# Cross attention: TensorE transposes the low half of 36 units in steps without another item, the DMA their high half alone

## What is computed

```python
def _L1_xattn_ref(q, k, v, wq, wk, wv, wo):      # N_HEADS 16, HEAD_DIM 64
    qh = (q @ wq.T).reshape(B, Sq, N_HEADS, HEAD_DIM).transpose(0, 2, 1, 3)
    kh = (k @ wk.T).reshape(B, Sk, N_HEADS, HEAD_DIM).transpose(0, 2, 1, 3)
    vh = (v @ wv.T).reshape(B, Sk, N_HEADS, HEAD_DIM).transpose(0, 2, 1, 3)
    scores = jnp.einsum('bhqd,bhkd->bhqk', qh, kh) / jnp.sqrt(jnp.float32(HEAD_DIM))
    attn = jax.nn.softmax(scores, axis=-1)
    ctx = jnp.einsum('bhqk,bhkd->bhqd', attn, vh)
    ctx = ctx.transpose(0, 2, 1, 3).reshape(B, Sq, N_HEADS * HEAD_DIM)
    return ctx @ wo.T
```

## Time and profile before

| | us |
|---|---|
| median of 3 runs | 3689.03 (3686.04 to 3690.8) |
| profiled execution | 3689.56 |
| its span | 3687.8 |
| PE / DVE / ACT / POOL busy in the span | 3077.8 / 2698.4 / 2332.4 / 1058.7 |
| DMA transposes | 512 of L1998, 96 of L267 |
| mean granted TensorE clock | 0.928 of full |

### The profile page before, as it was taken

One profiled execution on the slowest core, in us unless ns is written; L12 is line 12 of the kernel. 1 busy time (PEld: TensorE's weight loads), 2 busy tenths in 40 slices (PEclk: granted clock), 3 DMA queues, 4 the chain that ended last, 5 costly groups with the idle time before them and its releaser, 6 DMA issues. The chain is left out here.

```text
span 3687.8 us, 77444 instructions
## 1 busy us (share of the span) xinstructions
PE 3077.8 (83%) x30696; PEld 1830.7 (50%) x30836; DVE 2698.4 (73%) x4017; ACT 2332.4 (63%) x4361; POOL 1058.7 (29%) x1854
## 2 busy tenths in 40 slices
PE   6999999878998755899688878998799879998823
PEld 3647474555665443444345544555455545555411
DVE  4848483777897665444379888888788888889788
ACT  3838374676786534333268877778777777788534
POOL 2232322156537235233122222222222222222122
PEclk9999999988998877999899999999999999999956
DMA  4050504266265375344399999999999999999843
GB/s 156 21 170 2 171 14 136 65 221 203 77 183 164 100 255 192 93 128 123 104 208 194 195 202 202 202 198 191 213 196 198 194 214 195 199 201 196 161 153 129
DMA packets 1346682, 591.77 MB, mean 160 GB/s; under 512 B 1181202, under 2 KB 1267858, under 8 KB 1343764
## 3 DMA queue, kind: packets, MB, share of 16 engines
q1 hardware_dynamic: 1342292, 570.03, 70.0%
q0 software_dynamic: 4032, 16.78, 1.2%
HBM read 183.63 MB, written 109.45 MB: 79 GB/s over the span
## 5 line engine op out<-in xcount | busy, mean ns | idle before, releaser
L2259 DVE SCALAR_TENSOR_TENSOR ca_halves<-ca_probs,ca_inv,ca_halves 128x1024 f16<-128x1024 f32 x512 | 655.1, 1279 | 138.8 <-ACT ca_halves L2187 132.0
L2187 ACT ACTIVATE ca_halves<-ca_probs,ca_inv 128x1024 f16<-128x1024 f32 x512 | 586.1, 1145 | 151.6 <-DMA ca_pt<-ca_halves 145.9
L2253 DVE TENSOR_REDUCE ca_neg_max<-banks 128x1 f32<-128x1024 f32 x512 | 623.1, 1217 | 65.2 <-PE banks L2056 63.5
L2179 ACT ACTIVATE ca_probs<-banks,ca_neg_max 128x1024 f32<-128x1024 f32 x512 | 567.7, 1109 | 82.0 <-DVE ca_neg_max L2253 79.3
L2056 PE MATMUL banks<-ca_kt,ca_qt 64*128 64x512 f16 x3072 | 388.7, 387 | 102.3 <-ACT ca_probs L2179 100.8
L2022 POOL TENSOR_SCALAR ca_inv<-ca_total 128x1 f32<-128x1 f32 x512 | 97.6, 191 | 1225.5 <-ACT ca_probs L2179 1225.5
L2076 PE MATMUL banks<-ca_pt,ca_v 128*64 128x256 f16 x6144 | 392.1, 278 | 18.4 <-DMA ca_pt<-ca_halves 18.4
L2076 PEld LDWEIGHTS banks<-ca_pt,ca_v 128*64 128x64 f16 x6144 | 322.3, 111 | 120.2 <-issue 104.6
L2025 POOL TENSOR_TENSOR ca_inv<-ca_inv,ca_minus_one 128x1 f32<-128x1 f32 x512 | 280.4, 548 | 42.6
L2056 PEld LDWEIGHTS banks<-ca_kt,ca_qt 64*128 64x128 f16 x3072 | 133.7, 95 | 297.5 <-issue 121.3
L2037 PE MATMUL banks<-ca_ct,ca_w 128*128 128x512 f16 x768 | 180.9, 386 | 53.0 <-DVE ca_kt L2233 29.5
(11 more groups left out here) (303 smaller groups left out, 5635.7 us busy)
## 6 DMA issues: line engine op xcount, KB each, us to landing
ca_w<-ca_w_parts SPq DMA_DIRECT2D x32, 768.0 KB, 5.6
wa_v<-v_rows SPq DMA_DIRECT2D x44, 264.0 KB, 4.6
v_rows<-wa_v_stage SPq DMA_DIRECT2D x32, 264.0 KB, 2.2
wa_x<-in_x SPq DMA_DIRECT2D x32, 256.0 KB, 5.2
wa_ring<-in_x SPq DMA_DIRECT2D x32, 256.0 KB, 3.8
x_after_window_attention<-wa_ring SPq DMA_DIRECT2D x32, 256.0 KB, 3.3
ba_tokens<-wa_tok_turned SPq DMA_DIRECT2D x32, 256.0 KB, 3.7
ba_xt<-ba_tokens SPq DMA_DIRECT2D x32, 256.0 KB, 7.4
```

The lines of the kernel that those rows point to most:

```text
L2179: act.activation(probs[:, slot, :], scores(i), ACT.Exp, bias=neg_max[:, slot:slot + 1], accum_out=total[:, slot:slot + 1]).then_inc(exped, 1)
L2187: act.activation(halves[:, slot, 0, :], probs[:, slot, :], ACT.Copy, scale=inv[:, slot:slot + 1]).then_inc(split_hi, 1)
L2253: dve.tensor_reduce(out=neg_max[:, slot:slot + 1], in_=scores(i), axis=X_AXIS, op=ALU.max, negate=True).then_inc(maxed, 1)
L2259: dve.scalar_tensor_tensor(out=halves[:, slot, 1, :], in0=probs[:, slot, :], scalar=inv[:, slot:slot + 1], in1=halves[:, slot, 0, :], op0= ...
```

## The change

In steps 2 to 255 that have no item (`flip_at`), PE transposes the low half of the last step's first unit into the spare bank, eight 128x128 pieces, once that half is written. ACT copies the bank into ca_pt one step later, ahead of its second exponential. The DMA transposes the high half alone for these units. New waits: `weigh` also waits for the copies of its units, `spare_free` for the copies before, DVE's low half of unit i for the flip of unit i - 3 (the slot), and ACT's copy for the weighing that last read this place of ca_pt.

```diff
+        flip_at = {step: 2 * (step - 1) for step in range(2, STEPS)
+                   if not any(step in busy for busy in (qk_at, v_at, tile_at, partly_at))}
+        flipped_units = set(flip_at.values())
+        low_flipped, low_placed = sem("ca_low_flipped"), sem("ca_low_placed")
+        def flips_until(unit):
+            return sum(1 for u in flipped_units if u <= unit)
...
-                            sp.dma_start_transpose(pt[:, step % 4, h, :, :],
-                                                   halves[:, i % SLOTS, :, :].rearrange("p q s -> p (q s)")
+                            parts = 1 if i in flipped_units else 2
+                            sp.dma_start_transpose(pt[:, step % 4, h, 0:parts * NT, :],
+                                                   halves[:, i % SLOTS, 0:parts, :].rearrange("p q s -> p (q s)")
                                                    ).then_inc(turned[i % SLOTS], 16)
...
+                        if flips_until(4 * g + 3):
+                            pe.wait_ge(low_placed, flips_until(4 * g + 3))
...
+                    flips = sum(1 for at in flip_at if at < step)
+                    if flips:
+                        pe.wait_ge(low_placed, flips)
...
+                def flip_low(i):
+                    bank = psum[:, SPARE, :].bitcast(F16)
+                    pe.wait_ge(split_lo, i + 1)
+                    for kb in range(NT):
+                        last = pe.transpose(bank[:, kb * P:(kb + 1) * P],
+                                            halves[:, i % SLOTS, 1, kb * P:(kb + 1) * P], consts.ident_h[:, :])
+                    last.then_inc(low_flipped, 1)
...
                 def beside(step):
+                    if step in flip_at:
+                        spare_free(step)
+                        flip_low(flip_at[step])
...
                 def high_item(step):
+                    if step in flip_at:
+                        i = flip_at[step]
+                        act.wait_ge(low_flipped, flips_until(i))
+                        if step >= 5:
+                            act.wait_ge(weighted, (step - 5) // 2 + 1)
+                        act.activation(pt[:, (step - 1) % 4, 0, NT:2 * NT, :],
+                                       psum[:, SPARE, :].bitcast(F16).rearrange("p (k c) -> p k c", c=P),
+                                       ACT.Copy).then_inc(low_placed, 1)
...
                     dve.wait_ge(split_hi, i + 1)
+                    if i - SLOTS in flipped_units:
+                        dve.wait_ge(low_flipped, flips_until(i - SLOTS))
```

## The result

The changed kernel takes 3650.15 us (median of 5 runs, 3638.95 to 3663.97) against 3686.04 (5 runs, 3675.41 to 3690.8). The ratio is 0.9902, 95% interval 0.9883 to 0.9921. The forecast was 3679 us, with a range of 3664 to 3697; the change gained some 36 us where 10 were expected. The profiled execution took 3650.15 us, its span is 3648.2.

The account below looks back on a forecast made before the run. ACT and DVE were taken to pace each other, with DMA transposes bounding about 146 of cross attention's 1624 us. Terms +8 (A), -7 (B), -11 (C) sum to -10 us against 3689.56, so 3679 us, range 3664 to 3697.

Parts of the forecast that it names:

- class B: Step 5 of twelve ordinary turns, unit 8 behind the weights: 12 flips, transpose relief 1.03 us each, sum -7 us.
- Class A: Step 2 of the same twelve ordinary turns, unit 2: 12 flips, 0.68 us of copy exposed each, no relief, +8 us.
- Class C: Four steps in a row at each of three batch ends: 12 flips, SP relieved, copies hidden, -11 us.
- What bounds the kernel: Cross attention: transposes bound about 146 of 1624 us; elsewhere ACT and DVE pace each other and pay for added work.
- Rival 1: Too small to measure, about 3688 us: queue relieved by less than 1.03 us, after large loads time is the load's; 25%.
- Rival 2: Slower, about 3701 us: ACT with its copies bounds steps 3 and 6 of the turn, no relief behind the weights; 17%.
- Rival 3: Much faster, about 3654 us: DMA engines bound every step, so 36 x 1.03 = -37 us, less little; 8%.

Follow-up runs that it names:

- e5: Changed kernel with all 36 copies sent to a scratch tile and the DMA transposing both halves as before; ratio 1.0037 to the kernel before, stage 1622.5 us.
- e2: Kernel before with flips only in step 5 of the twelve ordinary turns (12 flips); ratio 0.9966, stage 1600.7 us.
- e16: Changed kernel without the twelve flips of step 2 (24 flips left); 3659.55 us, ratio 0.9931 to the kernel before, stage 1587.2 us.
- e17: Kernel before with flips only in step 5 of ordinary turns, plus 64 idle waits on PE ahead of the stage; stage 1601.4 us, one execution.
- e6: Changed kernel without PE's and ACT's added work, 35 low halves not transposed at all; ratio 0.9888 to the kernel before, stage 1576.8 us.

## Why the prediction was wrong

The step that failed is the pricing of a halved transpose behind a large load (class B): its relief was put at 1.03 us, the difference of two undisturbed issues, where the run shows 2.2 us. Class A, put at a loss of 8 us, was the smaller error. The table has the terms of the sum beside what was measured, the mean of the changed kernel over its four positions less that of the kernel before:

| us | forecast | measured |
|---|---|---|
| A and B, ordinary turns | +8 - 7 = +1 | -17.8 |
| C, turns at the batch ends | -11 | -14.5 |
| tile turns, no flips | 0 | +2.5 |
| stage | -10 | -29.7 |

- **What bounds the kernel**: right in the main. The waits moved where the rows had them, and the stage's gain is under their 146 us. That all work added to ACT outside these waits is paid was too strong: 36 us of copies cost 10.5 alone (e5).
- **36 flips, the copy 1.006 us, the half transpose 1.27 us**: right (36, 1.004 and 0.91 to the next start, 1.24).
- **Class B, -7 us**: the main error, a term of the sum that was sized too low. With B and without A (e2, e16, e17) the ordinary turns lost 14.4 to 14.8 us against the kernel before with the same waits (573.3 without, the mean of its two profiles, and 575.8 with 64), beyond the term's own end of -12. The issue behind the weights is not 2.30 us long: SP could not hand on the last of a full transpose until the weights had drained, as the 24 landings above show, and unit 9 stood behind it. A half one passed in 1.24. I had 2.41 us beside the term as its upper bound and took the value of the undisturbed rows; the bound itself stopped at the 2.30 us of a full transpose. Averaged over the twelve turns the issue of unit 8 fell from 4.39 to 1.25 us, 3.14 less. Unit 9 was issued 0.03 us after its low half in place of 2.24, but its issue rose from 2.34 to 3.32, so the two together fell from 6.73 to 4.57. ACT's two waits fell from 1.68 and 0.82 to 0.69 and 0.13. That it is room in a queue for which SP waits is inferred from these times; no run varied the room itself.
- **Class A, +8 us**: wrong. In step 3 the copies cost 0.32 to 0.34 us each (+3.8 to +4.1 us for twelve in every kernel with them), not 0.68, and step 4 gives it back (-3.0 to -5.4 in the kernels that also halve the transpose). I charged the shift of DVE's low half as if the next step began with it; in step 4 of turn 13 ACT waits 0.46 us for the DMA and DVE 0.55 for ACT in the kernel before. And I put the relief there at nothing, because SP waits for DVE. It does not behind unit 2: with the copies alone (e5) unit 3 was issued 0.57 us after its low half, with the transpose halved as well (the changed kernel) 0.05 us after it. ACT's wait for the DMA in step 4 was 0.35 us in the mean in e5 and 0.05 in the changed kernel, and step 4 gave back only 1.2 us in e5. So the relief in class A returned some 3 us over the twelve turns. Against the mean position of before (576 us) the ordinary turns of A alone are 578 and 575: about 0. The lower end of my range for A, +0, was nearest.
- **Class C, -11 us**: the mechanism was right and the size a little low. SP's eight issues at each place fell by 3.3 to 4.2 us, as 4 x 1.03 has it. The six turns lost 14.5 us in the mean of the positions, 9 to 19 at single ones, and 12.3 with C alone, against an end of -14.
- **Rival 1**, and with it the sum that goes by the rate in the Trainium skill, Advanced Engine Details and Errata, section X-Bar Transpose (0.7 us for 256 KB, an estimate): fell. The relief behind the weights was more than 1.03 us, not less. One thing in it was right: after a large load the time is the load's, only a half transpose escapes it.
- **Rival 2** (slower): not borne out, as B gained. A alone was a little slower than the kernel before in both runs (1.0026, 1.0019), but in the first more than half of it lay in turns without a flip, and the second is not told from the kernel before with the same 128 waits (1.0016).
- **Rival 3** had nearly the time (3654) by another way: halving returned 35 us in e6, yet not 1.03 at each of 36 places. Behind the weights it was 2.2 us of SP's time, at the batch ends about 1.0, and class A returned about 0.3 a flip.
- **What I did not see**: the position of PE's code. Idle waits ahead of the stage move it by up to 8 us for the same work, a quarter of what the change is worth. That the loads of code do this is the likely reason and not shown; no run had them away. Over four positions the change is worth -29.7 us of stage. In time the repeated runs say -34 and -36 without waits and -37 with 128; the single executions with 64 and 192 say -15 and -38, the -15 with a block attention of 535 us. Where the few us between stage and time lie the profiles do not tell. Of the 26 us by which the classes alone fell short of the whole, most stood in untouched turns; that no real interaction of a few us is left among them cannot be told from one to four positions each.

## What to carry to other kernels

What a smaller DMA relieves need not be its own issue time. Here it was the time for which a large load held the issuing engine: look at the issue that stands behind such a load, at when the load lands, and at what waits behind both. Work moved to a busy engine was cheap where that engine waits later on in the same turn (36 us of copies cost 7 to 10). And where a part of the change seems to act in places that it does not touch, repeat it with the code moved by some instructions before believing it.

## What the runs showed of the hardware

- A DMA transpose of 1024 columns was issued in 1.24 us even behind 768 KB of weights. One of 2048 columns took 4.39 us there, 3.35 behind 384 KB and 2.3 elsewhere, and its issue behind 768 KB ended 0.06 to 0.31 us before the weights landed.
- The hold is in part passed on: the full transpose behind the half one took 3.32 us to issue in place of 2.34.
- A code packet that starts within 3.5 us after a transpose's issue began goes with 0.9 us more of issue (3.00 against 2.09), and 64 to 192 idle instructions on PE moved the stage of an unchanged kernel from 1612 to between 1614 and 1620 us.
- Block attention, the same code in every kernel, took 516 to 519 us at a granted clock of 0.94 and 535 at 0.90.
